# Padding the last 64-row tile of the second shared expert to 128 rows, and 16 instead of 8 places for gathered rows

## The reference

```
xn2     = layernorm(x)                                    # 2048 x 256
logits  = xn2 @ router                                    # 8 experts, 2 of them per token
routed: expert e takes up to 640 tokens:  h = silu(gate) * up   (256 -> 2 x 176),  y_e = h @ w_down[e]
        y[token] += weight * y_e[slot of the token]       # one row of 256 per token and choice
shared  = (silu(xn2 @ Wgate) * (xn2 @ Wup)) @ shared_w_down     # hidden width 704
out     = x + layernorm(routed + shared)
```

## Time and profile before

| | |
|---|---|
| three runs | 798.91, 798.91, 800.09 us; median 798.91 |
| the profiled execution | 800.48 us, of which 798.5 us are the span from the first to the last instruction |
| busy: PE / DVE / POOL / ACT | 745.3 (93%) / 574.3 (72%) / 543.1 (68%) / 467.6 us (59%) |
| chain that ended last, over the whole span | PE 73%, DVE 11%, issue 7%, ACT 4%, POOL 2%, DMA 2% |
| granted TensorE clock, mean | 0.989 |

### The profile page before, as it was taken

How to read it: one execution, slowest core, us unless ns; L and a number is a source line. 1 busy time by engine, 2 the same in 40 slices (tenths; PEclk the granted TensorE clock), 3 DMA queues, 4 the chain that set the end, 5 groups by cost and what they waited for, 6 DMA issues and landing times.

```text
span 798.5 us, 14037 instructions
## 1 busy us (share of the span) xinstructions
PE 745.3 (93%) x4364; PEld 625.8 (78%) x4364; DVE 574.3 (72%) x1536; ACT 467.6 (59%) x1163; POOL 543.1 (68%) x459
## 2 busy tenths in 40 slices
PE   5799999999999999999999999998999989899992
PEld 4577788888888888887777888777778878898761
DVE  6967886768777767778887777898572357775685
ACT  5557776766676767666567666565623255653432
POOL 4457998787878887778888988778533534433663
PEclk9999999999999999999999999999999999999997
DMA  9411346422122222221222222221151134532332
GB/s 299 126 46 53 91 159 184 147 68 68 67 67 68 67 68 67 68 64 57 69 74 73 87 73 56 65 74 48 54 159 41 64 142 174 183 144 86 110 98 90
DMA packets 47748, 75.73 MB, mean 95 GB/s; under 512 B 9728, under 2 KB 24640, under 8 KB 47680
## 3 DMA queue, kind: packets, MB, share of 16 engines
q1 hardware_dynamic: 43504, 65.19, 25.9%
q0 software_dynamic: 3072, 8.39, 3.3%
q10 hardware_dynamic: 1104, 1.31, 0.5%
HBM read 57.71 MB, written 17.17 MB: 94 GB/s over the span
## 4 chain that ended last, share of the span: by engine, by line
PE 73%; DVE 11%; issue 7%; ACT 4%; POOL 2%; DMA 2%; DVEq 0%; ACTq 0%; POOLq 0%
PE ps L432 21%; PE ps L968 16%; PE ps L933 13%; PE ps L984 9%; PE ps L954 7%; PE ps L1130 5%; DVE q_sw L1312 1%; DVE q_sw L1311 1%; DVE hid_both L1643 1%; POOL slot_inputs L1784 1%; DVE hid_hi L1633 1%; POOL o_lo L1768 1%; DVE hid L1638 1%; DVE hid L1630 1%; DMA kvh_rows<-hc_t 1%
## 5 line engine op out<-in xcount | busy, mean ns | idle before, releaser
L968 PE MATMUL ps<-pt,vp 128*128 128x512 f32 (+3 forms) x512 | 149.5, 434 | 10.3 <-DVE q_sw L1312 10.1
L633 ACT ACTIVATE prob<-ps,neg_max 128x512 f32<-128x512 f32 (+3 forms) x256 | 132.5, 525 | 33.4 <-DVE neg_max L1321 30.6
L968 PEld LDWEIGHTS ps<-pt,vp 128*128 128x128 f32 x512 | 82.7, 190 | 59.9 <-issue 30.5
L1749 POOL TENSOR_TENSOR q_sw<-q_cos,q_sw 128x512 f32<-128x512 f32 x62 | 79.2, 1277 | 65.9 <-DVE q_cos L1313 65.8
L1321 DVE CUSTOM_DVE_ANT_0 ps<-ps,causal_row 128x512 f32<-128x512 f32 (+3 forms) x256 | 120.2, 511 | 4.6 <-PE ps L933 4.5
L642 ACT ACTIVATE pt<-ps,vcol 128x512 f32<-128x512 f32 x64 | 44.2, 690 | 109.4 <-PE ps L954 109.4
L1768 POOL TENSOR_TENSOR o_lo<-o_t,o_hi 128x512 fp32r<-128x512 f32 x64 | 84.4, 1318 | 33.4 <-ACT o_hi L671 33.4
L954 PE MATMUL ps<-id_f,prob 128*128 128x128 f32 x640 | 92.3, 275 | 0.9 <-ACT pt L642 0.9
L933 PE MATMUL ps<-k_hi,q_hi 128*128 128x512 f32 x248 | 86.6, 349 | 0.4 <-POOL q_lo L1753 0.3
L1340 DVE TENSOR_TENSOR o_t<-ps,inv_row 128x512 f32<-128x512 f32 x64 | 44.3, 692 | 52.5 <-PE ps L968 52.5
L1753 POOL TENSOR_TENSOR q_lo<-q_sw,q_hi 128x512 fp32r<-128x512 f32 x62 | 80.2, 1294 | 2.6 <-ACT q_hi L665 2.3
(11 more groups left out here) (218 smaller groups left out, 1942.3 us busy)
## 6 DMA issues: line engine op xcount, KB each, us to landing
kh_row<-kvh_rows SPq DMA_DIRECT2D x64, 256.0 KB, 3.2
inv_row<-inverse_sums SPq DMA_DIRECT2D x64, 256.0 KB, 3.1
slot_inputs<-zeros SPq DMA_DIRECT2D x8, 640.0 KB, 4.9
xg<-slot_inputs SPq DMA_DIRECT2D x8, 640.0 KB, 4.5
slot_outputs<-yo SPq DMA_DIRECT2D x8, 640.0 KB, 3.3
up_raw<-in_w_up_dram SPq DMA_DIRECT2D x8, 368.0 KB, 4.5
wo_raw<-in_wout_dram SPq DMA_DIRECT2D x4, 512.0 KB, 7.9
dn_sb<-in_w_dn_dram SPq DMA_DIRECT2D x8, 256.0 KB, 3.5
```

The source lines that it names most:

```text
L633: ins = act.activation(prob[:, i % 2, ROW_AT[nt]:ROW_AT[nt] + w], ps_s[bank][:, at:at + w], ACT.Exp, scale=-1.0, bias=neg_max[:, i % 2, nt ...
L968: ins = pe.matmul(ps_qo[:, mt * P:SEQ], vp[:, b * TPB + mt, :], pt[:, i % 2, cols], start=(mt == 0), stop=(mt == PT_BANKS[-1][-1]))
L1749: pool.tensor_tensor(q_sw[:], q_cos[:], q_sw[:], ALU.add).then_inc(q_sum_ready, 1)
```

## The change

In `shared_down` every matmul uses all 128 partitions of `s_hid` and `sdn_sb`. For that DVE writes zeros into the unused upper 64 partitions of the third tile of the second part: once in `sdn_sb` before the routed experts, and in both buffers of `s_hid` after them, behind `split_shared(1)`. PE waits for the three writes (`shared_padded`) ahead of `shared_down(4)`. Apart from that, the tile `got` has 16 places in place of 8, and so also 16 semaphores.

```diff
@@ -175,7 +175,7 @@
         xn2_after = place("xn2", R1, [TILES, E])
-        GR = 8
+        GR = 16
         got = place("got", R1, [GR, E])
@@ -309,6 +309,7 @@
         gu_psum, silu_ready, gu_free = sem("gu_psum"), sem("silu_ready"), sem("gu_free")
+        shared_padded = sem("shared_padded")
@@ -1119,6 +1120,8 @@
             def shared_down(j):
                 n = j // B
                 pe.wait_ge(s_hid_ready, (j + 1) * SH)
+                if j == B:
+                    pe.wait_ge(shared_padded, 3)
                 for half in range(2):
@@ -1128,7 +1131,7 @@
                         for i in range(SH):
                             ins = pe.matmul(ps[6 + half][:, q * E:(q + 1) * E],
-                                            s_hid[0:SHW[n][i], j % 2, i, t * P:(t + 1) * P], sdn_sb[0:SHW[n][i], n, i, :],
+                                            s_hid[:, j % 2, i, t * P:(t + 1) * P], sdn_sb[:, n, i, :],
                                             start=(i == 0), stop=(i == SH - 1))
@@ -1646,6 +1649,7 @@
             dve.sem_inc(gu_free, 2)
+            dve.memset(sdn_sb[SHW[1][SH - 1]:, 1, SH - 1, :], 0.0).then_inc(shared_padded, 1)
             dve.memset(dn2_lo[0:LO + H2, :].bitcast(F32), 0.0).then_inc(pad_ready, 1)
@@ -1654,6 +1658,8 @@
             expert_steps(NE - 2, True)
             split_shared(1)
+            for r in range(2):
+                dve.memset(s_hid[SHW[1][SH - 1]:, r, SH - 1, :], 0.0).then_inc(shared_padded, 1)
```

## The result

The changed kernel takes 794.12 us, the median of six runs (792.51 to 795.18), against 800.10 us for the kernel before in six runs (798.91 to 800.97): a ratio of 0.9926 with a 95% interval of 0.9910 to 0.9942. It is faster by 6.0 us in the medians. I had forecast 791.7 us with a range up to 793.7, so the time lies outside the range by 0.4 us. The forecast gain of 7.2 us lies at the edge of the interval (4.6 to 7.2 us). The profiled execution took 792.51 us with a span of 790.5 us, 2.0 us less, the same distance as before.

What follows compares the result with a forecast made beforehand. The last stage was taken as bound by PE until about 776.8 us, then POOL's gathers until 786.6. Padding and places together moved the statistics from 786.59 to 779.35: 798.91 - 7.2 = 791.7 us, range 789.9 to 793.7.

Steps and rivals of the forecast that it cites:

- Padding on PE: In `shared_down`, 128 rows in all tiles save 1.47 us for each of four steps, 5.9 us on PE.
- What reaches the end: At the sums of `shared_down`, DVE and ACT's loop of 13.37 us lets only 1.6 of 5.9 us through.
- The places: With 16 places for gathers, POOL never waits for a place; 5.8 us from the places alone.
- The additions: Zero writes on DVE: `s_hid` 0.3 to 0.6 us each, `sdn_sb` about 0.27 us, all covered by waits.
- The meeting of both: Last gather landing at 778.5 nearly ties with DVE's last additions; statistics of sequence 2 at 779.35, gain 7.2 us.
- five times 0.27 and three times 0.15: Extra time of POOL's gathers beside runs of additions and `add_x`: 1.8 us, last gather starting at 775.7.
- on the scale of the median: Whole kernel: the 7.2 us gain taken from the 798.91 us median, giving 791.7 us.
- 0.5 lower: Whole kernel: a median falling 0.5 lower, part of the main case's low end of 790.6 us.
- The first (loop with more slack): Last stage: gathers not slowed, or DVE and ACT's loop has more slack; 9.4 us less, 789.5 us; chance 6%.
- The second (padding brings nothing): `shared_down`: idle time not caused by 64 rows; 5.8 us from the places alone, 793.1 us; chance 4%.
- The third: POOL's gathers: every one slowed to 1.28 us of work; only 3.0 us less, 795.9 us; chance 5%.
- The fourth: POOL's gathers: an unbroken stream backs up, making the kernel slower, 805 us at 2 us each; chance 2%.

Runs made afterwards that it cites:

- run without additions: Changed kernel without the additions of the first two sequences' routed rows (16 of the 32); one run, 789.11 us, last stage 61.6 us.
- writes-only kernel: Kernel before plus the three zero writes and PE's wait, still 64 rows and 8 places; ratio 0.9996, 799.09 us, last stage 69.3 us.
- second profile of the same kernel: Changed kernel run again unchanged, beside the kernel before; ratio 0.9910, 792.27 us, last stage 61.7 us.
- short loop: Changed kernel with DVE reordered: from the second sequence, half the additions precede the hidden tiles, and the end is reordered; ratio 0.9878, 790.09 us.
- POOL held back: Short loop with POOL's four additions of x for sequence 2 waiting for all 32 of DVE's gathered-row additions; ratio 0.9887, 790.49 us.
- gaps between additions: Changed kernel with every addition of gathered rows waiting for the end of the one before; one run, 797.30 us, last stage 66.8 us.

## Why the prediction was wrong where it was, and right where it was

**Padding on PE: right, and a little more than forecast.** No 64-row form is left, and the pace of the steps falls from 13.58 us (742.92 to 756.50 before) to 11.99 us (741.37 to 753.36). That is 1.59 us for a step, where I had 1.47. The step itself, from its start to that of the next work, takes 4.99 us in the second part (741.37 to 746.36) and not the 5.18 us of the first part, from which I took it. That it is the 64 rows that cost, and not less than 128, the run with 96 rows shows.

**What reaches the end: right.** I had 1.6 us for the padding alone, by a loop of DVE and ACT of 13.37 us with 0.2 us of slack. The padding-only kernel gained 1.6 us in the stage, the turns are 13.27 us, and the run without additions shows whose loop it is. In the times of the stage, the second half of `shared_sum(6)` was forecast at 46.0 us and came at about 45.7 (772.76 + 0.60 - 727.63 = 45.7).

One reading behind this was wrong, though no number hangs on it. I had the string of gathers in the kernel before start with five gathers, released by the addition at 777.43. The gather at 777.99 is the 28th and needs twenty additions; 24 were done by 775.9, and it starts 0.30 us after the one before it like its neighbours. The wait that counted is that of the 25th, for the first addition of the run from 772.52 on:

```profile
773.78 1.28 POOL L1877 DMA_INDIRECT got<-slot_outputs,at_out  x1 [2.98 <-DVE y_sb L1665]
```

So eight gathers lay behind DVE's third run of additions, and DVE's sum at 776.82, which waits for PE, was on no path to them. The releaser in brackets is an inference of the profile; the count in the code decides. The forecast survives because that run of additions moves by the same 1.6 us as the sum: it starts 43.3 us after the start of the stage before, and 41.7 us after it in the padding-only kernel.

**The places: right.** POOL never waited for one. Alone they bring 5.7 us; I had 5.8.

**The additions: right.** The two writes of `s_hid` took 1.02 us, ahead of 1.99 us of waiting; the writes-only kernel is equal to the kernel before.

**The meeting of both: mis-sized.** I put the last gather's start 1.8 us later for slow gathers, 46.5 us after the start of the stage, and its landing 2.8 us on. In the profile after it was 47.2 us and 3.16 us, so that the statistics began at 50.9 us instead of 50.2. The term "five times 0.27 and three times 0.15", 1.8 us, measured 2.4 us: up to the last one's start two gathers took 0.80 us more than 1.01, and four others 0.16 to 0.26 us more. It missed the 1.81 us that a gather can take within a run. In the second profile of the same kernel the last started at 46.3 us and the stage was 0.4 us shorter than forecast (61.7 against 62.1). The forecast of the stage lies between the two.

**The step that failed is "on the scale of the median", together with that term.** The time came out 2.4 us above the forecast, in two halves of equal size. I took 798.91 us, the median of three runs, as the level of the kernel before; six runs have it at 800.10 us, 1.2 us higher. And the gain was 6.0 us in the medians instead of 7.2, another 1.2 us, of which the profile shows 0.8 us in the last stage, by the slow gathers and the late landing. Either half alone would have left the time in the range: 800.10 - 7.2 = 792.9 us, or 798.91 - 6.0 = 792.9 us.

The range gave the level only "0.5 lower" and nothing higher, although the profiled execution of the same kernel, 800.48 us, lay 1.57 us above it. The level's other medians were 799.63, 800.40 and 799.28 us, and single runs of it spread from 797.4 to 802.3 us. The changed kernel's two groups of six gave 794.12 and 792.27 us. A forecast of 0.9910 (791.7 over 798.91) stands against 0.9926 and 0.9910 measured; that the second agrees to the last digit is luck, with an interval from 0.9891 to 0.9928. The start of the last stage varied by 6 us over the fourteen profiles, and the writes-only kernel (730.54, ratio 0.9996) shows that the writes do not move it. The range should have been a range of the ratio, carried to a level that is itself uncertain by up to 1.5 us.

**The rivals.** The first (loop with more slack) is refuted by the 13.27 us. The second (padding brings nothing) by the padding-only kernel, ratio 0.9964 with an interval that leaves out 1. The loader's idle time at each change is what costs here, and not the load with 64 rows, which takes 184 ns in the mean against 189 ns with 128. The Trainium skill ("TensorE: Matmul & The Clock Gate", Why this matters for your kernels) says that a single matmul over 32 rows takes as long as one over 128. With 64 rows the trace of the kernel before comes near to it, 428 ns in the mean against 399 ns, and the rule does not reach the idle time between them. The third happened in a small way: 1.81 us in some gathers, not 1.28 us in all. The first, the gathers not slowed, is refuted by these as well. The fourth did not: 32 gathers ran without a pause.

## What to carry to other kernels

A resource freed on the busiest engine is worth only its slack to the next loop: look at how long the follower waits for it (0.20 us here), not at how long it is busy. Where a queue of fetches waits for places, lay out times of need and times of issue side by side; the places are enough once the waits for them are over in time: 12, with one wait of 0.53 us left, did as well as 16 here, and no number between 8 and 12 was tried. Where the profile names a releaser for a wait of the usual length, count in the code whether the wait can have been one. And judge a change of under 1% by the stage it touches, aligned at the start of that stage, and by ratios on one chip, not by absolute medians of three runs.

## What the runs showed of the hardware

- **A change between 64 and 128 rows leaves the weight loader idle for 0.33 us; one between 96 or 112 and 128 rows does not.** There are eight changes in a step, and PE's pace falls from 13.58 to 11.99 us without them, so each costs PE about 0.2 us (an estimate: 1.59 us over eight). The product has more zeros in it and is faster.
- **Additions with two inputs in SBUF, back to back on DVE, hold up a gather's issue on POOL**: 1.8 us instead of 1.0 where it starts 0.72 to 0.74 us after the run does (743.54 against 742.80, 770.10 against 769.36), 1.0 where it starts 0.40 us after (756.48 against 756.08), and at most 1.24 us once each addition waits for the one before. Most gathers beside a run keep their 1.01 us (757.79, for one), so where in the run a gather starts matters. In the short loop two took 2.01 us. The Trainium skill ("SBUF — State Buffer", SBUF: two separate sides) names DVE's two-port modes as what starves such a DMA. The operation here is a `scalar_tensor_tensor` on f32, whose own time (3.37 us for eight) did not change; in which mode it ran no run here shows, so the delay is measured and its cause is open.
- **The same additions and POOL's `tensor_tensor` slow each other**: 1.32 and 1.89 us for a pair instead of 0.85 and 0.88, and 3.34 instead of 2.77 us for POOL's four. With POOL held back both were gone.
- **An idle time of 2.9 us may or may not lower the granted clock.** PE before and in `shared_down(7)`, in the first and in the second profile of the changed kernel (window, length, PE busy, granted clock, DMA share, GB/s):

```profile
770.60:773.60 3.00, 0.10 (x1) 0.96 0.28 79
773.60:781.00 7.40, 6.98 (x24) 0.79 0.20 53
```
```profile
771.60:774.60 3.00, 0.05 (x2) 1.00 0.33 101
774.60:780.20 5.60, 5.41 (x24) 1.00 0.16 47
```

After the same 2.9 us of idling the granted clock was 0.79 in the mean of the step in the one, so part of it ran at the lower level of 1.2 GHz, and stayed at 2.4 GHz in the other: 6.98 or 5.42 us. Neither was on the path, as DVE reads the second half later (783.85 in the first). Of the six profiles with 2.87 to 2.95 us of idling there, the step took 6.98 to 7.11 us in three and 5.42 us in three; after 1.56 us of idling (no additions for two sequences) it took 5.42 us, after 6.70 us (gaps between additions) 8.38 us.
